# A constant's buffer made 192 bytes wider, so that all buffers allocated behind it move up

## What is computed

```python
xn = layernorm(x)
x = x + L0_attn(xn) + L0_ffn(xn)        # low-rank state scan; silu(xn W1) * (xn W3), Hadamard, W2
xn = layernorm(x)
x = x + L1_attn(xn) + L1_ffn(xn)        # causal attention, 16 heads of 32; silu(gate) * up, kept 2 of 4, w_down
```

## The kernel before

| buffers | distance |
|---|---|
| `x_hi`, `x_lo`, `ident`, `wo`, `o_hi`/`o_lo` of row blocks 0 to 2 | 0 |
| `raw`, `res`, `gu`, `h_hi`, `h_lo`, `d_hi`, `d_lo`, `w_hi`, `w_lo`, `stack`, `o_hi`/`o_lo` of row block 3 | 64 |
| `v_hi`, `v_lo`, `prob` | 320 |

## Time and profile before

### The profile page before, as it was taken

One profiled execution on the slowest core, in us unless ns is written; L12 is line 12 of the kernel. 1 busy time (PEld: TensorE's weight loads), 2 busy tenths in 40 slices (PEclk: granted clock), 3 DMA queues, 4 the chain that ended last, 5 costly groups with the idle time before them and its releaser, 6 DMA issues. The chain is left out here.

```text
span 1749.1 us, 22683 instructions
## 1 busy us (share of the span) xinstructions
PE 1694.1 (97%) x8316; PEld 1334.2 (76%) x8316; DVE 1039.5 (59%) x1795; ACT 710.6 (41%) x1271; POOL 285.1 (16%) x281
## 2 busy tenths in 40 slices
PE   6999999999999999989999999989999999999998
PEld 3677888788788877767777777768888888888887
DVE  4321465564623454349999999956456455555775
ACT  4421322232213332239999999952222221222221
POOL 4201210310310102110000000031334021033220
PEclk9999999999999999999999999999999999999999
DMA  7200110100101037942555555432010010012243
GB/s 293 92 12 1 61 49 19 55 31 25 55 7 37 24 116 248 292 180 72 136 143 142 143 130 153 110 111 86 2 50 25 7 43 25 0 49 76 69 132 132
DMA packets 69662, 150.11 MB, mean 86 GB/s; under 512 B 9577, under 2 KB 18409, under 8 KB 68018
## 3 DMA queue, kind: packets, MB, share of 16 engines
q1 hardware_dynamic: 69554, 148.70, 27.4%
HBM read 102.13 MB, written 46.53 MB: 85 GB/s over the span
## 5 line engine op out<-in xcount | busy, mean ns | idle before, releaser
L1566 DVE TENSOR_TENSOR pt_lo<-p_turn,pt_hi 128x512 fp32r<-128x512 f32 (+3 forms) x384 | 200.6, 550 | 7.7 <-ACT pt_hi L1540 7.6
L1559 DVE TENSOR_REDUCE row_top<-p_score 128x1 f32<-128x128 f32 (+7 forms) x256 | 189.3, 750 | 15.4 <-PE p_score L1493 15.3
L1532 ACT ACTIVATE prob<-p_score,row_top 128x128 f32<-128x128 f32 (+7 forms) x256 | 185.9, 740 | 13.1 <-DVE row_top L1559 11.7
L1540 ACT ACTIVATE pt_hi<-p_turn 128x512 fp32r<-128x512 f32 (+3 forms) x384 | 181.9, 491 | 8.2 <-PE p_turn L1504 2.0
L1504 PE MATMUL p_turn<-ident,prob 128*128 128x128 f32 x1152 | 182.2, 276 | 1.1 <-DVE pt_lo L1566 0.8
L1025 DVE TENSOR_TENSOR hid<-hid,p_up 128x512 f32<-128x512 f32 x64 | 44.0, 687 | 224.8 <-PE p_up L490 209.1
L1895 DVE TENSOR_TENSOR e_hid<-e_hid,e_p_up 128x512 f32<-128x512 f32 x64 | 44.0, 688 | 207.7 <-PE e_p_up L1790 207.7
L1504 PEld LDWEIGHTS p_turn<-ident,prob 128*128 128x128 f32 x1152 | 129.8, 142 | 22.7 <-issue 8.7
L1519 PE MATMUL p_o<-pt_hi,v 128*65 128x512 f32 (+3 forms) x384 | 141.7, 376 | 2.8
L1491 PE MATMUL p_score<-stack 128*128 128x512 f32 (+3 forms) x384 | 127.9, 388 | 8.6 <-PEq L55 3.5
L772 ACT ACTIVATE hid<-p_gate 128x512 f32<-128x512 f32 x64 | 38.4, 599 | 223.5 <-PE p_gate L490 223.5
(11 more groups left out here) (269 smaller groups left out, 3931.0 us busy)
## 6 DMA issues: line engine op xcount, KB each, us to landing
stack<-qk_parked SPq DMA_DIRECT2D x256, 128.0 KB, 4.0
raw<-in_wgu SPq DMA_DIRECT2D x64, 256.0 KB, 2.8
qk_parked<-qk SPq DMA_DIRECT2D x16, 1024.0 KB, 4.0
v_parked<-v_out SPq DMA_DIRECT2D x16, 520.0 KB, 5.9
v<-v_parked SPq DMA_DIRECT2D x8, 1040.0 KB, 9.4
o_parked<-o_both SPq DMA_DIRECT2D x64, 128.0 KB
res<-in_x SPq DMA_DIRECT2D x8, 512.0 KB
rot<-in_w2t SPq DMA_DIRECT2D x4, 1024.0 KB, 7.5
```

What stands on the lines that cost most here:

```text
L1532: act.activation(row_at(h, r, 0, width_of(r)), p_score[:, r % 2, 0:width_of(r)], ACT.Exp, bias=top[:, r:r + 1]).then_inc(exped, 1)
L1540: act.activation(pt_hi[:, (BL * h + j) % PT, c0:W], p_turn[:, (BL * h + j) % TB, c0:W], ACT.Copy).then_inc(rounded, 1)
L1559: dve.tensor_reduce(top[:, r:r + 1], p_score[:, r % 2, 0:width_of(r)], AX_X, ALU.max, negate=True).then_inc(topped, 1)
L1566: dve.tensor_tensor(pt_lo[:, slot, c0:W], p_turn[:, (BL * h + j) % TB, c0:W], pt_hi[:, slot, c0:W].bitcast(F32), ALU.subtract).then_inc(sp ...
```

## The change

`qk_scale` holds one float per partition. Its buffer grows from 8 to 56 floats, 32 to 224 bytes. Only column 0 is loaded and read, before and after. `raw0_at` and every address behind it grow by 192 bytes; `ident`, `x_hi`, `x_lo`, `qk_bias` and what is placed in x's space stay.

```diff
--- before.py
+++ after.py
@@ -1977,7 +1977,7 @@
         x_lo = sb("x_lo", [P, TT, KD, W], F32R)
         spare = [at + 4 * KD * (T - W), at + 4 * KD * (2 * T - W)]
         handed = alloc(nc, ctx)[2]
-        qk_bias, qk_scale = sb("qk_bias", [P, HEADS // 2]), sb("qk_scale", [P, 8])
+        qk_bias, qk_scale = sb("qk_bias", [P, HEADS // 2]), sb("qk_scale", [P, 56])
         raw0_at = nc.sbuf_base
         sb("raw0_slab", [P, 3 * KD * P])
         w_at = nc.sbuf_base + 4 * (KD * P + KD * W + 8 * S)
```

## The result

The changed kernel takes 1736.45 us, the median of 4 runs (1735.48 to 1738.43), against 1756.27 us, the median of 4 runs of the kernel before. The ratio is 0.989, with a 95% interval from 0.9868 to 0.9912: 19.8 us or 1.1% faster, where 1734 us was forecast.

What follows compares the result with a forecast made beforehand. PE bounds the kernel outside attention: number of matmuls times a step that depends on operand distance. Terms 22.1 + 0.4 + 0.5 - 0.6 = 22.4, taken as 22 us off 1756.4, gave 1734 us, range 1727 to 1759.

Steps and rivals of the forecast that it cites:

- The sorting of steps by distance: PE steps by moving minus stationary address: 0 about 227 ns, -64 233.3 ns, 320 228.9 ns; equal distance cheapest seen.
- The modulus: For matmuls with x moving, new distance -256 counts as 0 modulo 256, so 226.7 ns; no row showed it.
- full gain: Matmuls with x moving drop to 226.7 ns; own range 1729 to 1740 us, chance 0.50.
- The main term, 22.1 us: Hidden, queries and keys, `project`, row block 3: 3350 matmuls with x moving, each 6.6 ns shorter; bounds 23.1 us and 0.
- The first steps behind each switch of family: Output blocks' first few steps lose their excess (227.3 against 226.7 ns), under 1 us over 32 units; 0.5 in the sum.
- What gives back, 0.6 us: PE's short waits on DVE and others in phase 1 grow by 0.08 us each, some eight such waits.
- sum of 22.4: Whole kernel: 22.1 + 0.4 + 0.5 - 0.6 us saved, taken as 22 us.
- The terms costed at nothing: Transposes, other engines (DVE 4 us either way at most), DMAs, and matmuls with both operands behind qk_scale: 0 each.
- The rule that spoke against: Trainium skill: independent read ports, one step for 512 columns (about 216 ns) whatever the addresses; time stays at 1756 us.
- No change: Rival: modulo 512 or more counts, or hidden products share another cause; hidden step 233 ns, 1756 us, chance 0.26.
- partial gain: Rival: distance 256 behaves as 320, 228.9 ns on 3350 matmuls, 14.7 us off, 1742 us; chance 0.13.
- the slower case: Rival: read streams meet more often at 256; hidden steps of phases 1 and 4 240 ns, 1778 us; chance 0.11.

Runs made afterwards that it cites:

- distance 512: Kernel before with qk_scale 120 floats wide instead of 8; 1734.88 us, ratio to before 0.9887.
- distance 288: Kernel before with qk_scale 64 floats wide instead of 8; 1751.31 us in a single execution.
- hidden at 192: Kernel before with qk_scale 40 floats wide instead of 8; 1743.13 us in a single execution.
- padded outputs: Changed kernel with a pad ahead of phase 4's output weights (e_d_hi): 192 bytes 1740.29 us, 64 bytes 1740.38 us, a single execution each.
- values and hidden at 128: Kernel before with qk_scale 24 floats wide instead of 8; 1755.61 us in a single execution.
- distances 320: Kernel before with qk_scale 72 floats wide instead of 8; 1753.56 us in a single execution.
- early mask load: Changed kernel with the load of mask_f issued before the values' stores instead of behind them; 1731.27 us, ratio to before 0.9866.

## Why the prediction was right

**What bounds, and the steps.** Reading PE by the starts in the timeline, not by busy time, was the step that carried it. PE is at 97% before and after; the gain does not show there. The sorting of steps by distance held in every run. With the values from before and after, moving minus stationary modulo 256:

| distance | step, ns | seen in |
|---|---|---|
| 0 | 226.7 | outputs; all families after the change; distance 512 |
| 32 | 233.3 | values at distance 288 |
| 64 | 228.9 to 229.4 | values before; hidden at 192; padded outputs |
| 128 | 232.4 to 233.2 | values and hidden at 128 |
| 192 (-64) | 233.2 to 233.5 | hidden before; values at 192; padded outputs |
| 224 (-32) | 233.4 | hidden at 288 |

**The modulus.** The prediction took 256 with no row at the new distance, between the bounds 226.7 and 233.3, and gave the full gain a chance of one half. It was a choice that came out, not a reading; distances 320 and 512 against 64 and 256 show it, and 128 shows that it is not smaller.

**The main term, 22.1 us.** As a sum of steps it was right. Matched one by one, the steps that run at the full clock in both executions are shorter by 8.5 us in the hidden products of phase 1, 0.2 in `project`, 2.1 in queries and keys, 10.1 in the hidden products of phase 4 and 0.3 in row block 3, 21.2 in all, and by 0.4 in the values. The first steps behind each switch of family, 0.5 us by the estimate, gave 0.5 in phase 4, and nothing in phase 1. Phase 4 kept all of its part: 10.1 + 0.3 + 0.5 = 10.9, and 0.5 more because fewer of its first steps fell in a stretch at the lower clock, which is luck; measured 11.4.

**What gives back, 0.6 us, was the term that was mis-sized.** The part that waits for no one but PE kept all of it; the parts with fixed ends kept little. In phase 1 the time up to each hidden matmul from the start before it sums to 364.3 us before and 354.5 after, 9.9 us less: 8.5 in steps, 0.8 in fewer steps at the lower clock, and 0.7 in a shorter wait ahead of the first unit, which lies before the phase as the table measures it. Of the rest, with 0.4 in `project` and smaller groups, some 4 us went: 1.6 for ACT at L423, 0.7 and 0.4 at L628 and L539, and about 1.5 in the stretch from 133.4 us. So 5.6 were left. In phase 2 the steps gave 2.1 + 0.4 us and the whole nothing: 0.6 went at L1285, 0.6 at the wait behind the mask load and about 1.6 in the stretch there. The prediction had looked at waits of PE, where that one is 2.0 us, and not behind it, where DVE waits over 10 us for a DMA; and it had no term for a clock that changes.

Attention came out 1.3 us longer with the same DVE and ACT busy time. Its start ran 13.7 us at the lower level instead of 10.2. Kernels with the old steps show 383 us with 13.7 too, and the one with the early mask load shows 381.5 with 10.2, so this is spread between executions and not the change.

Together this is the difference between 22 and the 15.5 us of the two profiled executions. The medians differ by 19.8, 2.6 us short of the sum of 22.4. The mean granted clock points at the same thing: it averages 0.9902 in eleven runs of before and 0.9887 in six of the change taken beside them. That is worth about 2 us as an estimate, since the fastest and the slowest run of before in the first set of experiments (1750.17 us at 0.993, 1762.37 at 0.985) lie 12.2 us apart for 0.008.

**The terms costed at nothing** were at nothing. Transposes: eight in 1.04 us as before (1.03 and 1.04). DVE: the groups of L918 and L925 at 685 and 691 ns, unchanged, though both SBUF operands of the latter moved. The same busy time in attention.

**The rule that spoke against.** Rows 5 and 6 already had steps of 227 and 233.3 ns for one shape, and the padded outputs moved from 226.7 to 233.5 ns by an address alone. The Trainium skill ("TensorE: Matmul & The Clock Gate", step 1 of Part 2) has weight load and moving operand on independent read ports; a step that depends on how the two operands lie to each other does not fit its conclusion that one takes nothing from the other, though no run here took the weight loads away. Whether banks of SBUF, the ports or something in the array is what they share was not tried and stays open.

**The rivals.** No change, partial gain and the slower case each named a step (233, 229, above 236), and each was excluded by the first unit of phase 4 in the new timeline. That a fourth distance would have a price of its own was true of 32 and 128, but none went above 233.5.

## What to carry to other kernels

Where PE is the bound and each matmul reloads its weights, read the step from one start to the next per family of matmuls, and compare families of one shape; a difference of 3% with no wait can be an address effect that a few bytes of padding remove. This was measured for 512 columns in float32 with 128 columns of weights; transposes of 128 columns took 109 ns a step at every distance they had here. Put the buffers that PE reads together at the same place modulo 256 bytes, and keep small buffers of 32 or 64 bytes from shifting what is allocated behind them. Then ask of each phase whether something with a fixed end stands in it, a DMA above all: a faster PE only waits longer there.

## What the runs showed that was not expected

The step is not symmetric and not monotonic in the distance: +32 costs 233.3 ns, +64 229, +128 232.4, -64 and -32 233.3. A distance of 32 bytes already costs as much as any that was measured.

Stretches at 1.2 GHz at waits of 2 to 3 us come and go between executions: the wait in the middle of phase 2, 2.65 to 2.7 us long, had one in both executions of the changed kernel and none with distance 512, whose phase 2 took 127.0 us instead of 128.1. At 1.6 us a stretch this is a part of the spread between runs of one kernel: in the thirteen runs of before mentioned above, the time by and large falls as the mean granted clock rises.
